# Top-64 attention with a three-step threshold search on one core: where GpSimd makes the second correction of a threshold

## The chip, the cores and the metric

The kernel runs on one core of a Trainium2 chip. A core has five engines that run side by side and meet only at semaphores: TensorE (PE in the profile) multiplies matrices, VectorE (DVE), ScalarE (ACT) and GpSimd (POOL) work on rows of on-chip memory, and SyncE (SP) issues transfers. Each engine runs its own instructions in the order in which the program hands them over. The metric is the time of one execution in microseconds (us), taken on the device; the times given are medians of several executions.

## What is computed

The reference takes x of 4 x 1024 x 256, applies half of a feed-forward layer, then attention, then half of the feed-forward layer again. Only the attention matters here. Cut to its core it reads:

```python
dots = jnp.einsum('bhid,bhjd->bhij', q, k) * QK_SCALE        # q and k normalised, 16 heads
dots = jnp.einsum('hg,bgij->bhij', W_pre_th, dots)           # heads mixed
dots = jnp.where(causal[None, None], mask_value, dots)       # 4 memory keys are always seen
vk = jax.lax.top_k(dots, TOPK)[0][..., -1:]                  # the 64th largest of a row
dots = jnp.where(dots < vk, mask_value, dots)
attn = jax.nn.softmax(dots, axis=-1)
attn = jnp.einsum('hg,bgij->bhij', W_post_th, attn)          # heads mixed again
out = jnp.einsum('bhij,bhjd->bhid', attn, v)
```

The hard part is `vk`: for each row of scores, its 64th largest value.

## The kernel before

Three stages run one after the other: a first stage (feed-forward and projections), the attention, and a last stage (feed-forward). The attention takes from about 905 us to about 3300 us of the profiled execution.

**Tiles and steps.** A tile is 8 queries of all 16 heads, so 128 rows, and as many columns as its last query can see: from 12 at the start of a sequence to 1028 at its end (`reach`, called n here). A sequence has 128 tiles, the four sequences have 512. A step k handles two tiles, an even and an odd one; there are 256 steps. Eight steps make a block of 128 queries, and eight blocks make a sequence. The widths grow from block to block and start again with the next sequence. Tiles with fewer than 76 columns need no search (`searched` is false for the first four steps of a sequence).

**The search.** ScalarE counts how many scores of a row lie above a guess: a pass of `Sign` over the tile with a running sum (line 1099, function `count(g, r)`, r from 0 to 3; each pass has a main instruction and a read of the sum). GpSimd turns the count into a better guess with two operations on 128 x 2 numbers: `move = cnt * factor` (line 1186), then, behind a semaphore on itself, `nt = move + base` (line 1187). This is `better(p, q)`, with q = 1, 2, 3 for the first, second and third correction. `better(p, q)` waits for both tiles' counts of round q-1, and ScalarE's counts of round q wait for its `nt`. After the fourth count (r = 3, written to `SG`) GpSimd works out how far off the count is and on which side (`off` and `sgn`, lines 1198 and 1200), and writes the scores with a sign and scaled to a tiny size into `W` (`signed(g)`, line 1209, the scaling pass, one per tile; this is the one wide pass of GpSimd in a step). VectorE puts the `SG` marks and `W` together (`sides(g)`, line 1354, one per tile, reading two arrays), takes the eight largest (`closest`, line 1361), and picks the right one (`picked`, lines 1369 and 1373). Then it cuts the exponentials at that threshold (`select`, line 1419).

**Which step works on which tiles.** The work is spread over steps by hand. In step k, ScalarE does in this order: the fourth counts of pair k-2, the copies `AT` of the mixed weights (line 1122) for the even tile of pair k-5, the second counts (r = 1) of pair k-1, the exponentials and copies of older pairs, the third counts (r = 2) of pair k-1, and the first counts (r = 0) of pair k. GpSimd does: third correction of pair k-2, first correction of pair k-1, the sides of pair k-2, two scaling passes of pair k-2, the second correction of pair k-1, then small work and two passes `kr` (line 1242), then the first guess of pair k (lines 1174 and 1180), which waits for VectorE's copies `D` of that pair (line 1340). VectorE does: `D` of pair k's even tile, `sides` of both tiles of pair k-2, `D` of the odd tile, `closest`, `picked`, and two `select`, with copies of new scores `Sn` (line 1329) in between. TensorE makes scores (lines 963 and 964), mixes heads (line 977), turns and mixes the weights (line 1004) and multiplies with the values (line 1032).

**What the scaling passes wait for.** `signed` of the even tile and of the odd tile wait for `sgn` and for the buffers `W` that `picked` has freed. `sides` of each tile waits for its own scaling pass through the semaphore `v`.

## Time and profile before

| | us |
|---|---|
| median of 3 executions | 3618.76 |
| lowest and highest of them | 3610.93 and 3638.0 |
| the profiled execution, its time | 3616.38 |
| the profiled execution, its span | 3614.0 |

The profile is of one execution. Its page gives for each engine the time in which it was busy, and groups of instructions with their count, busy time, mean duration and idle time just before them. The sum of the prediction is made against the 3616.38 us of the profiled execution; the median is 2.4 us (0.07%) above it. A row of the timeline begins with the start in us from the span's start and the duration in us; rows of one engine that follow each other with the same line are merged and counted (x2); where a pair is shown with x1 too, that answer was cut before the second began. Windows are given for three blocks of the third sequence, each of 8 steps from the start of the fourth counts of its first pair; a row has the window, its length, each engine's busy time with its count of instructions, and at the end the granted TensorE clock (1 is full), the share of DMA and its GB/s.

### The profile page before, as it was taken

What the parts mean: (1) busy time and instruction counts of PE and PEld (TensorE: products, weight loads), DVE (VectorE), ACT (ScalarE), POOL (GpSimd) and SP (SyncE); (2) the same over time, 40 slices, a digit from 0 to 9 for tenths busy, and PEclk for the clock granted to TensorE, in tenths of its full rate; (3) what the DMA queues carried; (4) which work ended last, traced back from release to release, by engine and by line L of the source; (5) the groups of instructions that cost most, each with busy time, mean ns of one, the idle gap of its engine ahead of it and who ended that gap; (6) DMA issues with size and microseconds to landing.
All of it is one profiled execution on the core that took longest, in us unless ns stands there. A gap on an engine that the chain in (4) does not pass through costs nothing. (4 is left out here: it accounts for less than half of the span.)

```text
span 3614.0 us, 73990 instructions
## 1 busy us (share of the span) xinstructions
PE 3186.2 (88%) x22950; PEld 2118.9 (59%) x22950; DVE 2795.0 (77%) x6342; ACT 2567.5 (71%) x5953; POOL 2380.7 (66%) x6267
## 2 busy tenths in 40 slices
PE   7999999997788898878999888889988899987898
PEld 4445454443556666755666665566676566666566
DVE  6677766667688999778999867899986888985354
ACT  3444544443688999778899967899986888896221
POOL 2666666655777767688776768776767876674232
PEclk9999999998699999989999998999998999999899
DMA  3223222224456665346666435566534566641110
GB/s 121 99 82 111 105 88 88 82 82 153 135 164 177 187 182 128 90 145 179 178 187 175 100 109 153 170 193 182 152 86 129 168 180 178 180 105 46 38 36 29
DMA packets 363391, 467.04 MB, mean 129 GB/s; under 512 B 29460, under 2 KB 295060, under 8 KB 362520
## 3 DMA queue, kind: packets, MB, share of 16 engines
q1 hardware_dynamic: 362904, 461.54, 43.5%
q8 instruction: 185, 3.03, 0.4%
q14 instruction: 302, 2.47, 0.3%
HBM read 227.09 MB, written 234.36 MB: 128 GB/s over the span
## 5 line engine op out<-in xcount | busy, mean ns | idle before, releaser
L1099 ACT ACTIVATE junk<-D,nt 128x76 int8<-128x76 f32 (+62 forms) x1440 | 1070.2, 747 | 98.4 <-POOL nt L1187 65.5
L1004 PE MATMUL banks<-kr,E 128*128 128x128 f32 (+1 forms) x4672 | 702.9, 299 | 111.1 <-ACT AT L1122 64.6
L1004 PEld LDWEIGHTS banks<-kr,E 128*128 128x128 f32 (+1 forms) x4672 | 602.2, 202 | 258.5 <-issue 154.2
L977 PE MATMUL banks<-Sg,kpre 128*128 128x109 f32 (+51 forms) x1568 | 603.6, 493 | 23.3 <-POOL maskb L1256 13.0
L1329 DVE COPY Sn<-banks 128x686 f32<-128x686 f32 (+11 forms) x440 | 375.9, 854 | 165.7 <-PE banks L964 130.2
L1354 DVE SCALAR_TENSOR_TENSOR W<-SG,sgn,W 128x76 f32<-128x76 int8 (+14 forms) x480 | 413.1, 900 | 104.1 <-POOL W L1209 103.5
L963 PE MATMUL banks<-kT,qT 64*128 64x343 f32 (+11 forms) x880 | 390.3, 525 | 103.6 <-DVE Sn L1329 97.5
L1122 ACT ACTIVATE AT<-banks 128x512 f32<-128x512 f32 (+3 forms) x768 | 344.8, 479 | 185.2 <-PE banks L1004 184.3
L585 DVE RECIPROCAL a_share<-a_share 128x512 f32<-128x512 f32 x128 | 419.9, 3324 | 70.3 <-POOL a_share L529 36.6
L1032 PE MATMUL banks<-AT,V 128*64 128x64 f32 x9216 | 392.8, 233 | 81.9 <-issue 71.5
L1032 PEld LDWEIGHTS banks<-AT,V 128*64 128x64 f32 x9216 | 323.1, 142 | 156.0 <-issue 138.1
L1419 DVE SCALAR_TENSOR_TENSOR E<-D,vk,E 128x12 f32<-128x12 f32 (+56 forms) x512 | 394.5, 779 | 3.1 <-ACT E L1109 1.5
L1099 ACT ACTIVATE SG<-D,nt 128x76 int8<-128x76 f32 (+14 forms) x480 | 357.0, 745 | 50.8 <-DVE hit L1369 48.4
L964 PE MATMUL banks<-kT,qT 64*128 64x343 f32 (+11 forms) x880 | 390.7, 526 | 0.0
L1209 POOL TENSOR_SCALAR W<-D,sgn 128x76 f32<-128x76 f32 (+14 forms) x480 | 376.2, 793 | 0.4
L1109 ACT ACTIVATE E<-D,least 128x12 f32<-128x12 f32 (+56 forms) x512 | 369.3, 721 | 9.6 <-POOL E L1236 6.5
L1340 DVE TENSOR_SCALAR_CACHE_REDUCE D<-banks 128x13 f32<-128x13 f32 (+62 forms) x504 | 339.4, 674 | 40.8 <-PE banks L981 40.3
L977 PEld LDWEIGHTS banks<-Sg,kpre 128*128 128x128 f32 x1568 | 267.0, 205 | 169.3 <-issue 116.2
L1186 POOL TENSOR_TENSOR move<-cnt,tab 128x2 f32<-128x2 f32 x720 | 224.0, 311 | 182.5 <-ACT junk L1099 177.8
L1361 DVE MAX8 m<-W 128x8 f32<-128x76 f32 (+14 forms) x480 | 326.7, 721 | 22.0 <-issue 19.5
L1099 ACT ACTIVATION_READ_ACCUMULATOR junk<-D,nt 128x1 f32 x1440 | 275.4, 191 | 0.0
L529 POOL TENSOR_SCALAR a_share<-a_share 128x512 f32<-128x512 f32 x128 | 190.3, 1487 | 122.0 <-ACT a_share L440 122.0
(195 smaller groups left out, 5710.8 us busy)
## 6 DMA issues: line engine op xcount, KB each, us to landing
score_scratch<-Sn SPq DMA_DIRECT2D x96, 343.0 KB, 3.4
q_scratch<-a_share SPq DMA_DIRECT2D x32, 512.0 KB, 2.7
v_scratch<-a_share SPq DMA_DIRECT2D x32, 512.0 KB, 3.6
k_scratch<-a_share SPq DMA_DIRECT2D x32, 512.0 KB, 2.7
gate_scratch<-a_share SPq DMA_DIRECT2D x32, 512.0 KB, 2.8
kT<-k_scratch SPq DMA_DIRECT2D x32, 512.0 KB, 4.8
gateT<-gate_scratch SPq DMA_DIRECT2D x32, 512.0 KB, 9.8
qT<-q_scratch SPq DMA_DIRECT2D x31, 512.0 KB, 6.4
```

The costliest lines, as they stand in the source:

```text
L585: nc.vector.reciprocal(ri[:, c % 2, :], rr[:, c % 2, :]).then_inc(s["inv"], 1)
L963: nc.tensor.matmul(ps[0][:, 0:c1 - c0], qT[0:DH, p, :], kT[0:DH, p, c0:c1], start=True, stop=True)
L964: nc.tensor.matmul(ps[1][:, 0:c1 - c0], qT[DH:P, p, :], kT[DH:P, p, c0:c1], start=True, stop=True).then_inc(s["s_ps"], 1)
L977: out = nc.tensor.matmul(bank[:, 0:c], kpre[:].rearrange("p h r -> p (h r)"), Sg[:, g % 3, c0:c1], start=True, stop=not diagonal)
L1004: out = nc.tensor.matmul(ps[5 + i % 2][0:rows, c % 4 * P:(c % 4 + 1) * P], E[:, g % 4, c * P:c * P + rows], kr[:, g % 4, :], start=True, s ...
L1032: out = nc.tensor.matmul(into, V[:, c, h * DH:(h + 1) * DH], rows, start=(c == 0), stop=(c == ib and (ib > 0 or hb % 2 == 0)))
L1099: nc.scalar.activation(out, D[:, e, 1:1 + n], ACT.Sign, bias=nt[:, r, e:e + 1], scale=-1.0, accum_out=cnt[:, r, e:e + 1]).then_inc(s[f"cnt ...
L1109: nc.scalar.activation(E[:, g % 4, 0:n], D[:, e, 1:1 + n], ACT.Exp, bias=least[:, e:e + 1], scale=-1.0).then_inc(s["exp"], 1)
L1209: ts(W[:, g % 2, 0:n], D[:, g % 8, 1:1 + n], sgn[:, g % 8:g % 8 + 1], -SMALL, ALU.mult, ALU.mult).then_inc(s["v"], 1)
L1329: nc.vector.tensor_copy(Sn[:, i % 2, :, 0:c1 - c0], banks[:, 0:2, 0:c1 - c0]).then_inc(s["s_sb"], 1)
L1354: nc.vector.scalar_tensor_tensor(out=W[:, h, 0:n], in0=SG[:, h, 0:n], scalar=sgn[:, e:e + 1], in1=W[:, h, 0:n], op0=ALU.is_equal, op1=ALU. ...
L1419: nc.vector.scalar_tensor_tensor(out=E[:, g % 4, 0:n], in0=D[:, g % 8, 1:1 + n], scalar=vk[:, g % 8:g % 8 + 1], in1=E[:, g % 4, 0:n], op0= ...
```

## The change

One call changes its place in GpSimd's step. The second correction of pair k-1 stood behind both scaling passes of pair k-2; now it stands between them.

```diff
                 if searched(k - 2):
                     signed(2 * (k - 2))
-                    signed(2 * (k - 2) + 1)
                 if searched(k - 1):
                     better(k - 1, 2)
+                if searched(k - 2):
+                    signed(2 * (k - 2) + 1)
                 if searched(k - 2):
                     distance(k - 2)
```

No instruction is added or removed, and no wait changes. What moves can be seen in GpSimd's order at two places of a sequence. The first is the step whose scaling passes are 188 and 196 columns wide (a difference, + is new):

```order
 L1192 TENSOR_TENSOR base<-nt,tab 128x2
 L1209 TENSOR_SCALAR W<-D,sgn 128x188
+L1186 TENSOR_TENSOR move<-cnt,tab 128x2
+L1187 TENSOR_TENSOR nt<-move,base 128x2
 L1209 TENSOR_SCALAR W<-D,sgn 128x196
-L1186 TENSOR_TENSOR move<-cnt,tab 128x2
-L1187 TENSOR_TENSOR nt<-move,base 128x2
 L1215 TENSOR_TENSOR pos<-off,sgn 128x2
 L1242 TENSOR_SCALAR kr<-kpost,rinv 128x128
```

The odd tile's scaling pass now stands behind two small operations, the first of which waits for ScalarE's second counts of the next pair. The same happens in every step with a search. At the step with passes of 492 and 500 columns, ScalarE's order, which is the same before and now, shows who waits for the moved `nt`: the two counts of 508 and 516 columns that follow the exponentials (`E`).

```order
L1099 ACTIVATE SG,cnt<-D,nt 128x492
L1099 ACTIVATE SG,cnt<-D,nt 128x500
L1122 ACTIVATE AT<-banks 128x64x8
L1099 ACTIVATE junk,cnt<-D,nt 128x508
L1099 ACTIVATE junk,cnt<-D,nt 128x516
L1109 ACTIVATE E<-D,least 128x476
L1122 ACTIVATE AT<-banks 128x64x8
L1109 ACTIVATE E<-D,least 128x484
L1099 ACTIVATE junk,cnt<-D,nt 128x508
L1099 ACTIVATE junk,cnt<-D,nt 128x516
```

The first pair of 508 and 516 is the second count (r = 1), which the moved correction reads; the last pair is the third count (r = 2), which waits for what it makes.

## Rows read from the trace of the kernel before

**Rows 1.** The page: busy us, share of the span and instructions of each engine
```profile
PE 3186.2 (88%) x22950; PEld 2118.9 (59%) x22950; DVE 2795.0 (77%) x6342; ACT 2567.5 (71%) x5953; POOL 2380.7 (66%) x6267
```
**Rows 2.** Waits of the whole span: us in total, times, longest us
```profile
ACT junk L1099 <- POOL nt L1187: 65.5, 98, 1.3
ACT AT L1122 <- PE banks L1004: 184.3, 149, 5.2
POOL move L1186 <- ACT junk L1099: 177.8, 287, 2.6
DVE W L1354 <- POOL W L1209: 103.5, 79, 2.5
```
**Rows 3.** Groups by line: busy us, mean ns | idle us before, releasers
```profile
L1187 POOL TENSOR_TENSOR nt<-move,base 128x2 f32<-128x2 f32 x720 | 227.6, 316 | 56.4
L1354 DVE SCALAR_TENSOR_TENSOR W<-SG,sgn,W 128x76 f32<-128x76 int8 (+14 forms) x480 | 413.1, 900 | 104.1 <-POOL W L1209 103.5
```
**Rows 4.** Windows, blocks 2, 4, 8: length, busy PE, PEld, DVE, ACT, POOL
```profile
2147.80:2202.10 54.30, 42.68 (x297) 30.77 (x294) 38.99 (x168) 41.05 (x161) 44.06 (x193) 0.78 0.49 142
2264.10:2334.40 70.30, 60.47 (x524) 41.95 (x522) 61.48 (x176) 60.44 (x161) 54.34 (x192) 0.95 0.60 174
2598.40:2686.10 87.70, 74.72 (x716) 58.25 (x715) 76.40 (x154) 85.79 (x154) 66.61 (x166) 0.92 0.41 98
```
**Rows 5.** GpSimd's and VectorE's waits in block 2 (2147.8 to 2202.1)
```profile
POOL move L1186 <- ACT junk L1099: 1.9, 1, 1.9
POOL nt L1174 <- DVE D L1340: 1.5, 3, 0.8
DVE W L1354 <- POOL W L1209: 4.7, 4, 2.0
```
**Rows 6.** VectorE's wait in block 8 (2598.4 to 2686.1)
```profile
DVE W L1354 <- POOL W L1209: 8.5, 6, 2.1
```
**Rows 7.** Timeline, a narrow step of block 2: GpSimd, then VectorE
```profile
2168.47 0.83 POOL L1209 TENSOR_SCALAR W<-D,sgn 128x188 f32<-128x188 f32 x2
2169.27 0.29 POOL L1186 TENSOR_TENSOR move<-cnt,tab 128x2 f32<-128x2 f32 x1
2169.85 0.19 POOL L1215 TENSOR_TENSOR pos<-off,sgn 128x2 f32<-128x2 f32 x1
2168.93 0.91 DVE L1354 SCALAR_TENSOR_TENSOR W<-SG,sgn,W 128x188 f32<-128x188 int8 x2 [1.18 <-POOL W L1209]
```
**Rows 8.** Timeline, a step of block 4: GpSimd, VectorE, ScalarE
```profile
2315.60 1.34 POOL L1209 TENSOR_SCALAR W<-D,sgn 128x492 f32<-128x492 f32 x2
2316.90 0.60 POOL L1186 TENSOR_TENSOR move<-cnt,tab 128x2 f32<-128x2 f32 x1
2317.58 0.57 POOL L1187 TENSOR_TENSOR nt<-move,base 128x2 f32<-128x2 f32 x1
2316.31 1.14 DVE L1354 SCALAR_TENSOR_TENSOR W<-SG,sgn,W 128x492 f32<-128x492 int8 x1 [1.66 <-POOL W L1209]
2316.31 1.79 DVE L1354 SCALAR_TENSOR_TENSOR W<-SG,sgn,W 128x492 f32<-128x492 int8 x2 [1.66 <-POOL W L1209]
2315.86 0.19 ACT L1099 ACTIVATION_READ_ACCUMULATOR junk<-D,nt 128x1 f32 x1
2318.19 0.72 ACT L1099 ACTIVATE junk<-D,nt 128x508 int8<-128x508 f32 x1 [0.49 <-POOL nt L1187]
```
**Rows 9.** Timeline, the last step of block 4: GpSimd, then VectorE
```profile
2323.78 1.36 POOL L1209 TENSOR_SCALAR W<-D,sgn 128x508 f32<-128x508 f32 x2
2327.72 0.19 POOL L1186 TENSOR_TENSOR move<-cnt,tab 128x2 f32<-128x2 f32 x1 [2.58 <-ACT junk L1099]
2329.55 1.41 DVE L1354 SCALAR_TENSOR_TENSOR W<-SG,sgn,W 128x508 f32<-128x508 int8 x2
```
**Rows 10.** Timeline, a wide step of block 8: GpSimd, VectorE, ScalarE
```profile
2651.19 2.14 POOL L1209 TENSOR_SCALAR W<-D,sgn 128x972 f32<-128x972 f32 x2
2652.30 3.19 DVE L1354 SCALAR_TENSOR_TENSOR W<-SG,sgn,W 128x972 f32<-128x972 int8 x2 [2.08 <-POOL W L1209]
2653.18 0.18 ACT L1099 ACTIVATION_READ_ACCUMULATOR junk<-D,nt 128x1 f32 x1
2656.77 0.19 POOL L1174 TENSOR_TENSOR nt<-D,tab 128x2 f32<-128x2 f32 x1 [0.22 <-DVE D L1340]
2658.41 1.11 ACT L1099 ACTIVATE junk<-D,nt 128x1004 int8<-128x1004 f32 x1
```

## The prediction

> **What bounds the kernel now.** The page first: TensorE is busy for 88% of the span, VectorE 77%, ScalarE 71%, GpSimd 66% [rows 1]. These are means over three stages. The change touches the attention alone, so I read that next, block by block, in the view of windows [rows 4]. Block 2 of a sequence (narrow tiles) takes 54.3 us for 8 steps: GpSimd is the busiest with 44.06 us, and the view of waits gives it only 1.9 + 1.5 us of waiting [rows 5]; the other 7 us are the gaps of its semaphores on itself. So GpSimd's own string of small operations sets the pace there. Block 4 takes 70.3 us, with TensorE, VectorE and ScalarE all at 60 to 61 us and GpSimd at 54: no engine is full, the pace comes from how they wait for each other. Block 8 takes 87.7 us with ScalarE at 85.79: there ScalarE is the bound. The view of waits over the span then says what is to be had and what is at stake [rows 2]: ScalarE waits 65.5 us in 98 places for a corrected threshold `nt`, which can be any of the three corrections, and VectorE waits 103.5 us in 79 places for a scaling pass.
>
> **What one step does, worked out at three widths.** The timeline of a step in block 4 shows the mechanism [rows 8]. The two scaling passes take 1.34 us, .67 each. VectorE's `sides` of the even tile is issued at 2316.31, just behind the even pass (2316.27), but takes 1.14 us and ends at 2317.45; a pair of `sides` of about that width with no GpSimd pass beside it takes 1.41 us, so .7 each [rows 9]. It stood still until the odd scaling pass ended at 2316.94. The small operations suffer the same way from the other side: `move` should take .19 us as in [rows 9] and takes .60, until 2317.50, .05 us behind the end of `sides`; `nt` takes .57. So a GpSimd operation and a `sides` exclude each other, whole instruction by whole instruction, and who comes first goes first. The Trainium skill says the same in "SBUF — State Buffer", section "SBUF: two separate sides": the port pair that both share is an exclusive lock held for the whole instruction; this trace agrees. That page also has a blocked GpSimd operation go on about 115 ns behind VectorE's end, where the row above shows 50; by its figure each of the handovers below would cost .07 us more, two in a step where VectorE waits.
>
> In the new order the same step goes: even pass to 2316.27; the second counts of the next pair were read at 2315.86 + .19 = 2316.05, so `move` waits for nothing and ends at about 2316.46; `sides` even takes the freed turn and ends at about 2316.46 + .51 = 2316.97 (.51 is what it took from 2316.94 to 2317.45); `nt` slips in behind it, about 2317.03 instead of 2317.58 + .57 = 2318.15; the odd pass ends at about 2317.72; `sides` odd at about 2318.28 instead of 2316.31 + 1.79 = 2318.10. So three things move: ScalarE's third count, which waited .49 us, waits no more; GpSimd is through its three operations and two passes about .4 us sooner; and VectorE is through `sides` .2 us later, now idle in the middle.
>
> At the narrow width [rows 7] the same walk gives: even pass to 2168.89, `move` to 2169.08, `sides` even about .27 to 2169.35, `nt` to 2169.40, odd pass .41 to 2169.81, so `pos` at about 2169.8 against 2169.85. The gain of GpSimd is .05 us, or .15 if `sides` is quicker than I scale it; I take .1.
>
> At the wide width [rows 10] the second counts are read only at 2653.18 + .18 = 2653.36, while the even pass ended at 2652.26. Now the moved wait holds the odd pass behind it: `move` and `nt` take to about 2653.85, the odd pass (1.07) to 2654.92, `sides` odd to about 2656.0 against 2652.30 + 3.19 = 2655.49, so .5 us later. What is late next is `D` of the odd tile and then GpSimd's first guess, at 2656.77 now. Its count starts on ScalarE at 2658.41, 1.4 us behind the guess's end at 2656.96, so .5 us of delay fits under the counts that ScalarE has to do anyway.
>
> **The sum.** Four terms, for the four sequences.
> 1. Narrow steps, about 10 in a sequence where GpSimd sets the pace, 40 in all, .1 us each: -4 us. The row of `nt` bounds it: its mean is 316 ns [rows 3] against the .19 us of an undisturbed small operation [rows 9], over 720 of them .126 x 720 = 91 us, of which a third, the second corrections, 30 us, and as much for `move`: 60 us if all blocking went and all of it lay on the path. The other end is 0: in 3 steps of block 2 GpSimd waits for `D` behind all this [rows 5], which comes no sooner.
> 2. ScalarE's waits for `nt`, 65.5 us at most [rows 2]. Nothing keeps them on the path: in block 4 ScalarE has 10 us of idle time in 70, and the next thing that it waits for is TensorE's work for `AT`, 184.3 us in all; what it gains at the third count it gives back there unless TensorE is fed sooner. Ends 0 and -65.5. I take a tenth, -6 us, since the blocks with the longest of these waits are those in which GpSimd, VectorE or TensorE sets the pace.
> 3. VectorE's later end of `sides`, where it was waiting for them: 79 places [rows 2], .2 us in the middle and .5 in wide ones, so 79 x .5 = +40 us at the most. In block 8 there are 6 in this sequence [rows 6], 24 in four, covered by ScalarE as worked out above; in block 2 there are 4 [rows 5], 16 in four, where GpSimd sets the pace. The other 39 at .3 make 12 us, and I take half of it, +6 us, since VectorE's next wait is often for TensorE.
> 4. Where VectorE comes late to `sides`, nothing is lost: GpSimd is through before. The last step of a block is the sharpest case [rows 9]: `move` waited 2.58 us for the counts, until 2327.72, and the odd pass, which ended at 2325.14, will now end at about 2327.72 + .19 + .28 + .69 = 2328.9. VectorE starts that pair of `sides` at 2329.55. The cover is .7 us; without it up to 3 us a block, 32 blocks, 96 us. I take 0.
>
> Together -4 - 6 + 6 = -4 us, so 3616.4 - 4 = 3612 us, 0.2% under the median of 3618.8. A measurement of this kernel can tell about 1% (36 us) from no change.
>
> **The rivals.**
> A. ScalarE's waits for `nt` are on the path after all, and most of them come back. For it: 98 waits, in the blocks in which all engines have gaps; ScalarE would run ahead and feed the next counts sooner. Against it: TensorE and VectorE are as busy as ScalarE in block 4 [rows 4]. All of it gives 3616 - 65.5 = 3551, half of it 3583. Chance .2, of which .13 beyond 1%.
> B. Slower. The moved wait holds the odd scaling pass, VectorE stands at `sides` odd with its `D`, `closest` and `select` queued behind, and TensorE and ScalarE wait for those. Price: 79 x .5 = 40 us, 3656. It decides as soon as each waiting step costs over .46 us (36 / 79) with no cover, or as the cover of .7 us in the last step of a block [rows 9] is used up. For it: GpSimd waits 177.8 us for counts at `move`, 287 times, so they are often not there when it asks, though these are all three corrections. Against it: the wide steps, where it costs .5, have 1.4 us of slack. Chance .17, of which .11 beyond 1%.
> C. The change does nothing because the counts arrive no sooner than the end of the odd pass. In block 8 the second counts come 1.1 us behind the even pass, the length of the odd one, and ScalarE does not wait for `nt`: there it is so. In the narrow and middle steps it is not [rows 8]. 3616 to 3619, chance .08.
>
> **How the numbers follow.** The forecast of small terms that nearly cancel has .55. Its own range is 3598 to 3630: term 2 at twice its value and term 1 at three times on one side, term 3 at its full 12 us and a few more on the other. The range for 8 in 10 reaches into A and B: 3586 to 3646. It leaves out about .11 of A and .07 of B. Faster by over 1% (under 3583): A's .13. Slower by over 1% (over 3655): B's .11. Within 1%: the rest, .76.
>
> **What would show it.** ScalarE's wait for `nt` of line 1187 falls from 65.5 us to under 20, and its wait for TensorE at `AT` rises from 184 by a good part of that: term 2. The mean of `sides` falls from 900 ns to about 750, since it no longer stands still inside the odd pass, and VectorE's wait for a scaling pass rises from 103.5 us to 150 or more, now with waits before odd tiles too: term 3. The mean of `nt` falls below 316 ns. GpSimd's wait for counts at `move` rises from 177.8 us. Block 2 gets shorter by about 1 us, block 8 keeps its 87.7 us within half a us. It is wrong if block 4 changes by more than 1.5 us, if block 8 gets longer, or if the last step of a block shows VectorE waiting at `sides` odd.

## The result, and the profile after

The change costs 0.6%. The median after is 3642.56 us (four executions, 3640.32 to 3644.83) against 3619.22 us before (four, 3610.93 to 3638.0); the ratio is 1.0057 with a 95% interval of 1.0033 to 1.0082, so 12 to 30 us. It lies inside the range of the prediction and within its band of 1%, but on the other side of zero: 4 us of gain were forecast, 23 us of loss came. The profiled execution took 3641.57 us with a span of 3639.3 (before 3616.38 and 3614.0).

The page of the kernel after, busy time of each engine (as [rows 1]), and from its groups by line (busy us, mean ns | idle us before, releasers; from line 1285 on, every line number is one higher than before) those that answer to [rows 3] and three more:

```profile
PE 3193.4 (88%) x22950; PEld 2120.6 (58%) x22950; DVE 2760.9 (76%) x6342; ACT 2572.7 (71%) x5953; POOL 2413.3 (66%) x6267
...
L1187 POOL TENSOR_TENSOR nt<-move,base 128x2 f32<-128x2 f32 x720 | 176.7, 245 | 56.3
L1355 DVE SCALAR_TENSOR_TENSOR W<-SG,sgn,W 128x76 f32<-128x76 int8 (+14 forms) x480 | 391.4, 834 | 200.7 <-POOL W L1209 200.1
L1242 POOL TENSOR_SCALAR kr<-kpost,rinv 128x128 f32<-128x128 f32 x512 | 311.7, 609 | 29.6 <-DVE rinv L1427 29.5
L1099 ACT ACTIVATE junk<-D,nt 128x76 int8<-128x76 f32 (+62 forms) x1440 | 1070.5, 746 | 117.2 <-POOL nt L1174 94.8 <-POOL nt L1187 18.8
L1099 ACT ACTIVATE SG<-D,nt 128x76 int8<-128x76 f32 (+14 forms) x480 | 356.9, 744 | 73.9 <-DVE hit L1370 72.8
```

The corrections got quicker (`nt` 316 to 245 ns) and so did `sides` (900 to 834 ns), but VectorE's idle time in front of `sides` went from 104.1 to 200.7 us. Busy and idle together, `sides` took 413.1 + 104.1 = 517 us of VectorE before and 592 us now: 75 us more, of which 23 reached the end. The row of `kr` is one that the prediction had left out: this pass, which stands behind the odd scaling pass, had 215.5 us and a mean of 422 ns before. Of the 206 waits before `sides`, 79 stand before the even tile, as many as before, and 127 before the odd tile, where there was none.

The waits of the whole span after (us, times, longest), as [rows 2]:

```profile
ACT AT L1122 <- PE banks L1004: 159.1, 143, 3.8
POOL move L1186 <- ACT junk L1099: 172.4, 288, 3.3
DVE W L1355 <- POOL W L1209: 200.1, 206, 2.3
ACT junk L1099 <- POOL nt L1174: 94.8, 144, 14.8
ACT junk L1099 <- POOL nt L1187: 18.8, 35, 1.0
ACT SG L1099 <- DVE hit L1370: 72.8, 113, 2.0
```

and three of the kernel before that the prediction did not use:

```profile
ACT junk L1099 <- POOL nt L1174: 29.6, 45, 14.2
ACT SG L1099 <- DVE hit L1369: 48.4, 80, 1.7
POOL nt L1174 <- DVE D L1340: 129.5, 99, 4.8
```

ScalarE's wait for a correction (`nt` of line 1187) fell from 65.5 to 18.8 us, as meant. But its wait for the first guess (`nt` of line 1174) rose from 29.6 to 94.8, and its wait for VectorE's `hit` from 48.4 to 72.8. So ScalarE starts its third counts sooner and then stands still at the first counts. VectorE's wait for a scaling pass rose to 200.1 us, in 206 places where there were 79.

Blocks 2, 4 and 8 of the third sequence after (length, busy PE, PEld, DVE, ACT, POOL; as [rows 4]):

```profile
2169.20:2223.70 54.50, 42.83 (x297) 30.64 (x296) 38.34 (x169) 41.14 (x161) 45.61 (x192) 0.81 0.50 141
2285.50:2355.90 70.40, 60.31 (x524) 41.86 (x522) 60.48 (x177) 60.64 (x162) 55.89 (x192) 0.95 0.59 174
2619.80:2709.90 90.10, 73.55 (x714) 57.02 (x712) 72.84 (x157) 86.43 (x152) 68.61 (x166) 0.92 0.39 95
```

Block 2 is .2 us longer, block 4 .1, block 8 2.4. GpSimd is busy 1.5 us more in each of the first two.

Three steps tell how. The step of block 4 with passes of 492 and 500 columns after, which answers to [rows 8] (start us, duration us, engine, line; in brackets the idle time before and what ended it):

```profile
2338.09 0.68 POOL L1209 TENSOR_SCALAR W<-D,sgn 128x492 f32<-128x492 f32 x1
2338.74 0.20 POOL L1186 TENSOR_TENSOR move<-cnt,tab 128x2 f32<-128x2 f32 x1
2338.81 0.73 DVE L1355 SCALAR_TENSOR_TENSOR W<-SG,sgn,W 128x492 f32<-128x492 int8 x1 [1.25 <-POOL W L1209]
2339.01 0.58 POOL L1187 TENSOR_TENSOR nt<-move,base 128x2 f32<-128x2 f32 x1
2339.58 0.68 POOL L1209 TENSOR_SCALAR W<-D,sgn 128x500 f32<-128x500 f32 x1
2340.22 0.19 POOL L1215 TENSOR_TENSOR pos<-off,sgn 128x2 f32<-128x2 f32 x1
2340.29 0.74 DVE L1355 SCALAR_TENSOR_TENSOR W<-SG,sgn,W 128x500 f32<-128x500 int8 x1 [0.75 <-POOL W L1209]
2340.39 0.87 POOL L1242 TENSOR_SCALAR kr<-kpost,rinv 128x128 f32<-128x128 f32 x1
```

Counted from the start of the even pass, `sides` of the odd tile ends at 2340.29 + .74 - 2338.09 = 2.94 us; before, at 2316.31 + 1.79 - 2315.60 = 2.50. That is .44 us later where the prediction had .2. Behind it GpSimd's `kr` pass now overlaps `sides` odd and takes .87 us.

The narrow step of block 2 with passes of 188 and 196 columns after, as [rows 7]:

```profile
2190.48 0.43 POOL L1209 TENSOR_SCALAR W<-D,sgn 128x188 f32<-128x188 f32 x1
2191.79 0.19 POOL L1215 TENSOR_TENSOR pos<-off,sgn 128x2 f32<-128x2 f32 x1
2191.86 0.42 DVE L1355 SCALAR_TENSOR_TENSOR W<-SG,sgn,W 128x196 f32<-128x196 int8 x1 [0.50 <-POOL W L1209]
2191.96 0.56 POOL L1242 TENSOR_SCALAR kr<-kpost,rinv 128x128 f32<-128x128 f32 x1
```

`pos` stands 2191.79 - 2190.48 = 1.31 us behind the start of the even pass, before it was 1.38: the .07 us that term 1 counted on are there, and `kr` takes them and more (.56 us, before .36). `sides` odd ends 1.80 us behind that start against 1.37, so .43 us late, much as in block 4.

The wide step with passes of 972 and 980 columns after, as [rows 10]; `SG` is the end of its fourth counts:

```profile
2671.35 1.05 POOL L1187 TENSOR_TENSOR nt<-move,base 128x2 f32<-128x2 f32 x1
2672.07 0.19 ACT L1099 ACTIVATION_READ_ACCUMULATOR SG<-D,nt 128x1 f32 x1
2674.12 1.08 POOL L1209 TENSOR_SCALAR W<-D,sgn 128x972 f32<-128x972 f32 x1
2675.51 1.01 POOL L1186 TENSOR_TENSOR move<-cnt,tab 128x2 f32<-128x2 f32 x1 [0.31 <-ACT junk L1099]
2677.89 1.24 DVE L1355 SCALAR_TENSOR_TENSOR W<-SG,sgn,W 128x980 f32<-128x980 int8 x1 [1.43 <-POOL W L1209]
2677.99 1.38 POOL L1242 TENSOR_SCALAR kr<-kpost,rinv 128x128 f32<-128x128 f32 x1
2680.40 0.19 POOL L1174 TENSOR_TENSOR nt<-D,tab 128x2 f32<-128x2 f32 x1 [0.52 <-DVE D L1341]
2680.63 1.13 ACT L1099 ACTIVATE junk<-D,nt 128x1004 int8<-128x1004 f32 x1
```

`sides` odd ends 5.01 us behind the start of the even pass, before 4.30. The first guess ends at 2680.59 and its count begins at 2680.63: of the 1.45 us that lay between them before [rows 10], .04 are left. Two rows of the kernel before, the end of the same fourth counts and the third count of this step, tell where they went:

```profile
2650.01 0.18 ACT L1099 ACTIVATION_READ_ACCUMULATOR SG<-D,nt 128x1 f32 x1
2656.20 1.10 ACT L1099 ACTIVATE junk<-D,nt 128x988 int8<-128x988 f32 x1
```

Behind the end of the fourth counts ScalarE's first counts begin at 8.22 us before (2658.41 - 2650.19) and 8.37 after (2680.63 - 2672.26), nearly the same. But the even pass begins at 1.00 before and 1.86 after, and the guess ends at 6.77 and 8.33. So GpSimd is .86 us late already when the step's passes begin, and .70 more are added in the step. The .86 come from the step before: VectorE's two `select`, which read two arrays as `sides` does, now fall later, and the second (2671.14 to 2672.34) blocks GpSimd's first correction (`nt`, 1.05 us above; .19 us before, at 2649.04).

**The mean over the steps.** Worked out from all records of the two traces, over the 222 steps whose neighbours have searches too, in us behind the end of a pair's fourth counts, which is the start of a step's work:

| | before | after |
|---|---|---|
| even scaling pass ends | 2.12 | 2.19 |
| second correction ends | 3.98 | 3.07 |
| odd scaling pass ends | 2.89 | 3.80 |
| `sides` odd ends | 4.68 | 5.05 |
| first guess ends | 5.97 | 6.16 |
| `hit` ends | 7.78 | 8.04 |
| third counts begin | 4.65 | 4.31 |
| first counts begin | 6.23 | 6.22 |
| the next step's fourth counts begin | 7.98 | 8.08 |

The third counts begin .34 us sooner, the first counts do not, since their guess is .19 us later; and the next step is .10 us later. Times 222 that is 22 us, about the whole loss.

**By block.** From one pair's fourth counts to the next, summed over the four sequences, the profiled execution after is longer than the one before by these us (22.9 together):

| block | 1 | 2 | 3 | 4 | 5 | 6 | 7 | 8 |
|---|---|---|---|---|---|---|---|---|
| after less before | 1.2 | .1 | 8.4 | 2.2 | .5 | -3.8 | 6.1 | 8.1 |

So blocks 3, 7 and 8 make the loss, and block 6 gains.

### The profile page after: what moved, and what is told of

Its sections match the earlier page's. It is cut to its first block and busy times, and to the rows that moved or that the text cites. A ratio compares the mean times of both kernels' runs of the same rounds, so it can differ in the third digit from the quotient of the medians.

```text
span 3639.3 us, 73990 instructions
## 1 busy us (share of the span) xinstructions
PE 3193.4 (88%) x22950; PEld 2120.6 (58%) x22950; DVE 2760.9 (76%) x6342; ACT 2572.7 (71%) x5953; POOL 2413.3 (66%) x6267
## 5 line engine op out<-in xcount | busy, mean ns | idle before, releaser
L1099 ACT ACTIVATE junk<-D,nt 128x76 int8<-128x76 f32 (+62 forms) x1440 | 1070.5, 746 | 117.2 <-POOL nt L1174 94.8
L1355 DVE SCALAR_TENSOR_TENSOR W<-SG,sgn,W 128x76 f32<-128x76 int8 (+14 forms) x480 | 391.4, 834 | 200.7 <-POOL W L1209 200.1
L1122 ACT ACTIVATE AT<-banks 128x512 f32<-128x512 f32 (+3 forms) x768 | 344.0, 477 | 160.1 <-PE banks L1004 159.1
L1099 ACT ACTIVATE SG<-D,nt 128x76 int8<-128x76 f32 (+14 forms) x480 | 356.9, 744 | 73.9 <-DVE hit L1370 72.8
L1032 PEld LDWEIGHTS banks<-AT,V 128*64 128x64 f32 x9216 | 322.6, 142 | 147.9 <-issue 128.6
L1242 POOL TENSOR_SCALAR kr<-kpost,rinv 128x128 f32<-128x128 f32 x512 | 311.7, 609 | 29.6 <-DVE rinv L1427 29.5
L1186 POOL TENSOR_TENSOR move<-cnt,tab 128x2 f32<-128x2 f32 x720 | 206.8, 287 | 178.1 <-ACT junk L1099 172.4
```

Source lines behind the costliest of these rows:

```text
L1032: out = nc.tensor.matmul(into, V[:, c, h * DH:(h + 1) * DH], rows, start=(c == 0), stop=(c == ib and (ib > 0 or hb % 2 == 0)))
L1099: nc.scalar.activation(out, D[:, e, 1:1 + n], ACT.Sign, bias=nt[:, r, e:e + 1], scale=-1.0, accum_out=cnt[:, r, e:e + 1]).then_inc(s[f"cnt ...
L1355: nc.vector.scalar_tensor_tensor(out=W[:, h, 0:n], in0=SG[:, h, 0:n], scalar=sgn[:, e:e + 1], in1=W[:, h, 0:n], op0=ALU.is_equal, op1=ALU. ...
```

## Experiments

Three theories stood at the start (their letters have nothing to do with those of the rivals above). **V**: VectorE comes late through `sides` odd, and what is queued behind it (`D`, `closest`, `hit`) holds ScalarE. **G**: GpSimd's `kr` pass, now blocked by `sides` odd, makes the first guess late, and that alone costs. **C**: the passes are held by the moved wait for the second counts. The ratios below are against the kernel before on the same chip, with 95% intervals. A step below is counted as in the table of means, from the end of a pair's fourth counts.

### The wait alone, and each half of the blocks

The kernel before, with nothing but the wait of the moved correction between the two passes:

```diff
                     signed(2 * (k - 2))
+                    if searched(k - 1):
+                        pool.wait_ge(s["cnt1"], 2 * FP[k - 1] + 2)
                     signed(2 * (k - 2) + 1)
```

> The kernel before, with one wait more: between the two scaling passes GpSimd waits for the second counts of the next pair, and the correction stays behind both passes. Theory C: this holds the odd pass as the change does, so most of the 23 us appear, 3630 to 3645, above all in blocks 7 and 8, where the counts come 0.3 to 1 us behind the even pass. Theories V and G in their form that the loss comes from the handovers between sides, the correction and kr: in blocks 1 to 5 the counts are there already, nothing changes; in blocks 7 and 8 sides even gets its turn in the wait, so some of it appears; 3618 to 3628.

3622.86 us, 0.9999 [0.9984, 1.0015]. Its waits:

```profile
DVE W L1356 <- POOL W L1209: 147.9, 131, 2.5
...
POOL W L1209 <- ACT junk L1099: 92.9, 105, 3.9
```

GpSimd stands 92.9 us at the odd pass, and nothing comes of it: the steps in which the pass is held by the counts are not those that cost. C falls as the cause of the whole. It also shows that 44 us more of waiting at `sides` (147.9 against 103.5) can be free, with a `sides` odd that ends .07 us later in the mean step.

The new order in blocks 7 and 8 alone, and, with `< 48` in place of `>= 48`, in blocks 1 to 6 alone:

```diff
+                between = (k - 2) % 64 >= 48
                 if searched(k - 2):
                     signed(2 * (k - 2))
+                    if not between:
+                        signed(2 * (k - 2) + 1)
                 if searched(k - 1):
                     better(k - 1, 2)
-                if searched(k - 2):
+                if searched(k - 2) and between:
                     signed(2 * (k - 2) + 1)
```

> The new order in blocks 7 and 8 of each sequence alone, the old one in blocks 1 to 6. Summed over steps of the two profiles the change costs 6 us in block 7 and 6.5 in block 8, plus about 4 in the steps at the turn of a sequence. If the cost of a block is its own: 3628 to 3636. If it is made elsewhere and only shows there: under 3624.

> The new order in blocks 1 to 6 alone, the old one in blocks 7 and 8. By the two profiles blocks 1 to 6 cost 1 + 0 + 8 + 2 + 1 - 4 = 8 us together: 3622 to 3630. Theory C says that nothing is lost where counts are there in time, so about 3619.

Blocks 7 and 8: 3631.78 us, 1.0034 [1.0018, 1.005]. Blocks 1 to 6: 3626.67 us, 1.0019 [1.0003, 1.0035]. The two losses of some 12 and 7 us add up to 19, near the 23 of the whole. The loss is not one of a single place. That the widest quarter of the steps has the larger part is likely, and the table by block says so, but the two intervals overlap.

### The repairs that V and G ask for

V says that `D` of the odd tile should not stand behind `sides` odd. So the new order with VectorE's `D` between its two `sides`:

```diff
                     sides(2 * (k - 2))
-                    sides(2 * (k - 2) + 1)
                 if k < S:
...
+                if searched(k - 2):
+                    sides(2 * (k - 2) + 1)
```

> The new order, and on VectorE the copy D of the odd tile of pair k ahead of sides of the odd tile of pair k-2, instead of behind it. Theory V (VectorE's path): the change costs its 23 us because sides odd now starts only when the late odd scaling pass is through, and D, the first guess and ScalarE's first count stand behind it; then D first fills VectorE's hole of 0.5 to 1.4 us, ScalarE's wait for the first guess (94.8 us) falls below 40 and the time comes back to 3615 to 3625. Theory G (GpSimd's path: the even kr pass stands still inside sides odd, 797 ns instead of 440, and the first guess stands behind it): kr still collides with sides odd, so at most a third comes back, 3635 to 3643. Theory C (the odd pass is held for the second counts): nothing comes back in the wide blocks.

3637.05 us, 1.0052 [1.0033, 1.0071]: 2 us better than the change by the ratios, 5 by the medians, which is not to be told from nothing. VectorE's wait for the passes fell to 117.5 us, and another took its place, for TensorE's sums (`flag`), 7 us in the kernel after:

```profile
DVE W L1355 <- POOL W L1209: 117.5, 116, 2.5
...
DVE flag L1337 <- PE banks L991: 94.3, 120, 3.7
```

This is a miss for V as it stood: it asked for 3615 to 3625 us and for ScalarE's wait for the first guess below 40 us, and that wait is 101.4 us. The trace shows why the test is weak. `sides` odd now ends later still (5.9 us into the step), the even `kr` pass is blocked by it as before (a mean of 569 ns, 797 after the change, 440 before), and GpSimd comes to the guess .69 us behind the end of `D` (.15 after the change). The run traded one hold-up for another.

The same edit on the old order is the control.

> The control to D first: the old order on GpSimd, and D of the odd tile between the two sides on VectorE. With the new order this took 5 us off. Here VectorE has no hole between its sides. Theory V: D and the first guess come 0.7 us sooner but sides odd, closest and picked later, 3615 to 3625. If D first costs by itself, because VectorE stands waiting for TensorE (95 us of waiting before flag in the run with the new order, 7 without), 3625 to 3635, and then it gave back more than 5 us in that run.

3640.97 us, 1.0072 [1.0054, 1.009]. So the repair costs 28 us by itself, above the range for it too, yet does not worsen the new order. V can live with that (the edit takes in one place what it gives back in another), but neither run speaks for V.

The `D` of the odd tile ahead of both `sides`, old order:

```diff
-                if searched(k - 2):
-                    sides(2 * (k - 2))
-                    sides(2 * (k - 2) + 1)
                 if k < S:
...
+                if searched(k - 2):
+                    sides(2 * (k - 2))
+                    sides(2 * (k - 2) + 1)
```

> The old order on GpSimd, and on VectorE D of the odd tile ahead of both sides. D reads the matmul's banks, not the shared port, so it can run beside the two scaling passes, in the time in which sides even stands still. If VectorE's standing still in sides even (1007 ns against 793 of sides odd, 51 us over 240 steps) is worth something, this is faster than both kernels, 3590 to 3615; if TensorE does not have the odd tile ready by then, VectorE waits for it with both sides behind, and it is slower, 3625 to 3650.

3747.16 us, 1.0358 [1.0332, 1.0384]. `flag` waits 342.2 us for TensorE; the wait for the passes is down to 12.1 us. It is far above both ranges named for it. Both places of the odd `D` ahead of the old one are worse.

G says that the guess must come ahead of `kr`. The new order with the first guess moved up:

```diff
-                if 0 <= k - 4 < S:
-                    spread(2 * (k - 4))
                 if searched(k - 1):
                     based(k - 1, 2)
-                if 0 <= k - 4 < S:
-                    spread(2 * (k - 4) + 1)
                 if searched(k):
...
+                if 0 <= k - 4 < S:
+                    spread(2 * (k - 4))
+                if 0 <= k - 4 < S:
+                    spread(2 * (k - 4) + 1)
```

> The new order, and on GpSimd the first guess of the next pair (lines 1174 and 1180) ahead of both kr passes instead of behind them. Theory G: the even kr pass, 797 ns instead of 440 because it stands still inside sides odd, holds the first guess and so ScalarE's first count (wait 94.8 us); with the guess in front of it the loss goes, 3619 to 3627. Theory V (sides odd itself is late, and D behind it): the guess has to wait for D anyway, kr is now held behind that wait, and the time stays at 3640 or gets worse, with TensorE waiting for kr.

3675.15 us, 1.0153 [1.0129, 1.0176], about 1% worse than the change. The guess has nothing before it and still ends 6.21 us into the step (6.16 after the change), because it waits for `D`:

```profile
POOL nt L1174 <- DVE D L1341: 298.0, 233, 17.5
```

So G falls: `kr` is stretched by half, but the guess was waiting for VectorE anyway. The trace of the kernel after says the same without the edit: there the guess begins .15 us behind the end of `D` in the mean (.25 before), and within .1 us of it in 163 of 232 steps (129 before). The control, the same edit on the old order:

> The control for the run before: the old order with the first guess ahead of both kr passes. Theory G: there kr hardly stood still (440 and 403 ns), so moving the guess changes little, 3612 to 3622. Theory V: the same. If this order costs by itself, for kr then waits behind D and TensorE behind kr, this run shows the cost and it has to be taken off the run before.

3628.24 us, 1.0033 [1.0015, 1.0051]; there the guess does come sooner (5.83 against 5.97), and the edit costs 11 us all the same, above the 3612 to 3622 us expected; that the late `kr` is the reason is not shown.

Both repairs on the new order:

> The new order with both repairs: D odd ahead of sides odd on VectorE, and the first guess ahead of kr on GpSimd. D first alone gave back 5 of 23 us (3637). If the first guess is what the loss runs through, by D and by kr together, both repairs give back more than their sum, 3612 to 3622. If the loss runs through sides odd itself to closest, picked and select, nothing more comes back than by D first, 3635 to 3645.

3642.95 us, 1.0067 [1.004, 1.0093]: as the change alone. ScalarE's wait for the first guess fell to 38.3 us, near the 29.6 of the old order, its wait for `hit` stayed at 73.7, and the time did not come back. By what was expected that speaks for a loss through `closest`, `picked` and `hit`, and not through the guess; but each repair costs time of its own in the old order (28 and 11 us), so the run doesn't decide it. It was run on another chip than the first repair, so it doesn't tell their shares.

### VectorE late, with GpSimd's order as it was

The cleanest test of V leaves GpSimd's order alone and puts a dead operation between VectorE's two `sides`, a `MAX8` over 384 columns whose result is overwritten:

```diff
                     sides(2 * (k - 2))
+                    nc.vector.max(m8[:, 2 * (k - 1) % 8, :], kpost[:].rearrange("p h r -> p (h r)").unsqueeze(1).broadcast_to([P, 3, H * R8]))
                     sides(2 * (k - 2) + 1)
```

> The old order; between the two sides of a step VectorE does one more operation of 384 columns that nothing reads (about 0.45 us by the row of MAX8, 0.72 us at 550 columns). It does not touch the port that GpSimd shares. So VectorE is through its pair of sides later by about what the change makes it (0.37 us in the mean of a step), and GpSimd's order is as before. Theory V (the cost of the change is only that VectorE ends its pair of sides later): 3636 to 3650. If the cost is made on GpSimd's side (kr, late scaling pass), then VectorE's gaps of over 1 us a step take this up: 3619 to 3626.

3655.16 us, 1.0115 [1.0098, 1.0132], so 42 us. Its groups and waits:

```profile
L1471 DVE MAX8 m<-kpost 128x8 f32<-128x384 f32 x240 | 132.0, 550 | 0.0
L1242 POOL TENSOR_SCALAR kr<-kpost,rinv 128x128 f32<-128x128 f32 x512 | 289.8, 567 | 32.2 <-DVE rinv L1426 31.6
...
ACT SG L1099 <- DVE hit L1369: 69.9, 115, 2.0
ACT junk L1099 <- POOL nt L1174: 69.7, 147, 14.9
```

The old order shows every sign of the change as soon as VectorE is late: `kr` 567 ns, ScalarE waiting for the first guess in 147 places (144 after the change) and for `hit` in 115 (113). In the mean of the steps the second correction even ends sooner than before (3.78), but `sides` odd ends at 5.16, the guess at 6.24, `hit` at 8.10, the next step begins at 8.14. So the stretched `kr` is a consequence of a late `sides` odd; that a late VectorE costs time is shown here, with `kr`'s part in it. That the inserted operation does not itself block GpSimd is in the traces: `MAX8` reads one operand, and in the kernel before GpSimd's `move` takes .19 us while one runs (2319.78). The Trainium skill, "SBUF — State Buffer", section "SBUF: two separate sides", has a VectorE operation take the shared port when it has two inputs in SBUF or runs in a two-port mode. The trace agrees: `sides` has two and excludes GpSimd (`move` .60 us in [rows 8]), `MAX8` has one and does not (.19).

The same with 128 columns, to see whether the price is proportional:

```diff
                     sides(2 * (k - 2))
+                    nc.vector.max(m8[:, 2 * (k - 1) % 8, :], kpost[:].rearrange("p h r -> p (h r)"))
                     sides(2 * (k - 2) + 1)
```

> The delay of VectorE between its two sides once more, with 128 columns in place of 384, so about 0.2 us in place of 0.45. Theory V with no slack at all: in proportion, 3630 to 3638. If the pair of sides has some slack in most steps, the small delay costs much less than in proportion, 3613 to 3624.

3629.48 us, 1.0019 [1.0007, 1.0031], so 7 us, for 283 ns of `MAX8` and a `sides` odd that ends .23 us later. With .48 us later and 42 us above, the first quarter of a us is nearly free and the next costs. A straight line between the two gives for the change's .37 us a loss of 7 + (.37 - .23) / (.48 - .23) x 35 = 27 us; 23 were measured. That is an estimate over two points, and its fit is in part luck, for by block the two kinds of delay do not cost the same (us over four sequences, as in the table by block):

| block | 1 | 2 | 3 | 4 | 5 | 6 | 7 | 8 |
|---|---|---|---|---|---|---|---|---|
| `MAX8` of 384 columns | 1.1 | 3.8 | 3.1 | 1.8 | 12.2 | 10.4 | 4.3 | 1.6 |
| the change | 1.2 | .1 | 8.4 | 2.2 | .5 | -3.8 | 6.1 | 8.1 |

In part this is how late `sides` odd is: in blocks 5 and 6 it ends .64 and .54 us later by the `MAX8`, .18 and .05 by the change. But in block 3 the two are about equally late (.33 and .38) and the change costs nearly three times as much, and in block 8 (.85 and 1.21) five times as much. So a late `sides` odd is a cause; that it is the only one is not shown. These are single profiled executions; with the new order in blocks 7 and 8 alone, blocks 1 to 6 differ by up to 1.5 us each from the kernel before, which gives a measure of the scatter.

### What the split costs, and what the early correction is worth

In the old order, the operation `pos`, which stands behind the passes with a wait of GpSimd on itself, put between them; the correction stays behind both:

```diff
                     signed(2 * (k - 2))
+                    distance(k - 2)
+                    pool.wait_ge(s["pos"], FP[k - 2] + 1)
                     signed(2 * (k - 2) + 1)
...
-                if searched(k - 2):
-                    distance(k - 2)
```

> The old order of the corrections, but the small operation pos (line 1215), which GpSimd did behind them anyway, stands between the two scaling passes, with a wait for its end, so that VectorE's sides even gets its turn there. The pair of passes is split as in the change; the correction does not come early and no count is waited for. Theory of the split: sides odd ends about 0.3 us later as in the change, and the time goes up by as much as by the change or more, since ScalarE gets nothing for it: 3638 to 3655. If the early correction itself does harm (ScalarE ahead of the others), this run stays at 3619 to 3626.

3644.28 us, 1.0082 [1.0066, 1.0099], so 31 us without any early correction. VectorE stands at the passes in 232 places, and ScalarE's wait for the correction grows too:

```profile
DVE W L1354 <- POOL W L1209: 193.1, 232, 2.5
...
ACT junk L1099 <- POOL nt L1187: 111.2, 124, 1.6
```

Here `sides` odd ends only .18 us later (4.86), but the correction .31 us later (4.29). The next test takes that apart: the correction later and the passes not. In the old order GpSimd's `base` for the second correction (line 1192) goes from ahead of the passes to behind them:

```diff
-                if searched(k - 1):
-                    based(k - 1, 1)
                 if searched(k - 2):
                     signed(2 * (k - 2))
...
                 if searched(k - 1):
+                    based(k - 1, 1)
                     better(k - 1, 2)
```

> The old order, but the small operation base1 (line 1192, 0.2 us), which stood ahead of both scaling passes, stands behind them, ahead of the second correction that needs it. Both passes and VectorE's pair of sides come 0.18 us sooner, the correction by nothing, GpSimd's work is the same. Theory V says that the time follows the end of the pair of sides in both directions: by the run with VectorE's delay (42 us for 0.45 us) up to 16 us less, so 3598 to 3613, with ScalarE's waits for hit and for the first guess lower. If the end of sides has slack on this side, so that only a delay counts: 3613 to 3620.

I had meant it to bring the passes forward. It did not: they end .02 us sooner, because most of the .19 us of `base` lay in the gap behind `sgn`, for which the pass waits (`sgn` ends at 2168.34, the pass begins at 2168.47 in the narrow step of the kernel before). Behind the passes it is blocked by `sides`, and the correction ends .36 us later (4.34). 3640.31 us, 1.0054 [1.0036, 1.0072]:

```profile
L1192 POOL TENSOR_TENSOR base<-nt,tab 128x2 f32<-128x2 f32 x480 | 164.6, 343 | 0.3
```

So a correction that comes .36 us later costs 17 to 20 us (with it the first guess comes .10 us later, so the price is not of the correction alone). What one that comes .91 us sooner brings, as in the change, no run measures: the estimate above would leave 4 us for it, and that is within its error.

The correction ahead of both passes, which needs no split:

```diff
-                if searched(k - 2):
-                    signed(2 * (k - 2))
                 if searched(k - 1):
                     better(k - 1, 2)
                 if searched(k - 2):
+                    signed(2 * (k - 2))
                     signed(2 * (k - 2) + 1)
```

> The second correction ahead of both scaling passes. The two passes are neighbours again, so sides even stands still inside the odd pass as in the kernel before, and nothing of the pair of sides is split; but both passes come later by the correction (0.47 us) and, in blocks 7 and 8, by the wait for the counts. Theory of the handovers (the loss is the split of the pair: three turns one after the other where there were two): no third turn here, so less lost than by the change in blocks 1 to 6, and a total of 3622 to 3635. Theory C: both passes held, worse than the change, over 3650.

3751.08 us, 1.0379 [1.0352, 1.0406], far above the 3622 to 3635 us that the theory of the handovers gave; it lies where C had put it (over 3650). The wait for the counts now holds both passes, and the even one ends 3.47 us into the step in place of 2.12:

```profile
POOL move L1186 <- ACT junk L1099: 313.7, 373, 2.6
...
ACT junk L1099 <- POOL nt L1174: 203.6, 196, 13.7
DVE W L1354 <- POOL W L1209: 250.1, 185, 4.1
```

### One instruction in place of two with a wait between

Perhaps the new place would pay with a correction that needs no semaphore between `move` and `nt`. It was written as one operation for each tile, with the factor and the base as pointers, in both orders:

```diff
-                chain(tt(move[:, q - 1, e], cnt[:, q - 1, e], tab[:, G1 + q - 1, t], ALU.mult))
-                tt(nt[:, q, e], move[:, q - 1, e], base[:, q - 1, e], ALU.add).then_inc(s[f"nt{q}"], 1)
+                for i in range(2):
+                    c, d = e.start + i, t.start + i
+                    last = ts(nt[:, q, c:c + 1], cnt[:, q - 1, c:c + 1], tab[:, G1 + q - 1, d:d + 1],
+                              base[:, q - 1, c:c + 1], ALU.mult, ALU.add)
+                last.then_inc(s[f"nt{q}"], 1)
```

> The old order; each correction is made by one operation for each of the two tiles (count times factor plus base, 128 x 1) instead of move and then nt on both tiles behind a semaphore on itself. GpSimd loses three waits on itself in a step, and the third count's threshold comes sooner with the pair of passes unsplit. The run with base1 behind the passes made that threshold 0.36 us later and cost 20 us. If the time follows the threshold in this direction too, 3590 to 3610; if only the end of VectorE's pair of sides counts, 3610 to 3622.

> The same with the new order. Two short operations back to back leave VectorE no gap in which sides even gets its turn ahead of nt, if the second is already waiting when the first ends; then the odd pass is held by only 0.3 us and one handover less. By theory V the change's cost of 23 us falls to 5 to 15 us against the run with the old order and the same operations. If VectorE still gets its turn between them, the cost stays at 20 us or more against that run.

Old order 3691.96 us, 1.0206 [1.0174, 1.0238]; new order 3722.55, 1.0285 [1.0257, 1.0314]. The two are 31 us apart, so the new place costs no less with this correction than with the old one, though no semaphore stands between its two operations: VectorE gets its turn all the same. And the form is dear, where a gain or no change had been expected. In the old order:

```profile
L1188 POOL TENSOR_SCALAR nt<-cnt,tab,base 128x1 f32<-128x1 f32 x1440 | 735.7, 520 | 133.4 <-ACT junk L1099 128.2 <-DVE hit L1372 1.0
```

1440 x 520 ns = 736 us stand where `move` and `nt` had 224 + 228 us and 56 us of gaps between them. No kernel that was run is clearly faster than the old order.

## Why the prediction was wrong

The step that failed is term 3 of the sum, VectorE's later end of `sides`: it was put at +6 us, with the wide steps of block 8 at nothing because ScalarE was to cover them. The runs showed 127 new waits before `sides` odd, 75 us more of VectorE's time at `sides`, and a loss of 23 us, of which blocks 7 and 8 have 14 by the profiles. Terms 1 and 2, together -10 us, did not come through to the end either. That the time stayed within 1% is no credit to the sum.

**What bounds the kernel** was read rightly, and so was the first part of the mechanism: a scaling pass and a `sides` exclude each other, `sides` even takes the freed turn, the correction slips in behind it, and VectorE is through later. Rival B had the mechanism of the loss, VectorE standing at `sides` odd with `D`, `closest` and `select` queued behind. It got .17 and a price of 40 us; 23 us are 60% of that.

**Term 3 failed in its price, its count and its cover.** The time of one was too small: .2 us in the middle was .44, .5 in the wide step was .7, and the narrow step, where I had none, lost .43. The prediction timed `sides` odd behind the odd pass with .56 us, from a `sides` that had been issued and was standing blocked (.51 us of it behind the block's end). But VectorE waits for the odd pass through a semaphore, is idle, and only then issues: .03 us for the semaphore and .74 for the whole operation, 2341.03 - 2340.26 = .77 us. This .21, and .05 that had come together up to the end of the odd pass, make the .26 between the .18 of the walk and the .44. The number of places was too small: 79 was the count of waits in the old order, where the odd pass comes straight behind the even one and never lets VectorE wait a second time. The new order adds 127 before the odd tile, 206 in all. The cover in the wide steps is answered under term 2. The last factor, that half is given back, was not too kind: of 75 us more on VectorE 23 reached the end. In the wide step the end of the odd pass, 3.74 us behind the start of the even one, came out as walked (3.73), but by luck: the counts were there .87 us sooner than in [rows 10], since GpSimd was late itself, and `sides` even, which had begun in the wait, then blocked `move` for most of its 1.01 us.

**Term 4 was right in its sharpest case and too broad.** In the last step of block 4 (as [rows 9]):

```profile
2349.18 0.20 POOL L1186 TENSOR_TENSOR move<-cnt,tab 128x2 f32<-128x2 f32 x1 [0.95 <-ACT junk L1099]
2349.63 0.70 POOL L1209 TENSOR_SCALAR W<-D,sgn 128x516 f32<-128x516 f32 x1
2351.00 1.54 DVE L1355 SCALAR_TENSOR_TENSOR W<-SG,sgn,W 128x508 f32<-128x508 int8 x2
```

The odd pass ends at 2350.33 and VectorE comes at 2351.00: the .7 us of cover are there. But the odd pass ends .91 us later in the mean step, and each VectorE that used to come within these .91 us without waiting now waits. "Nothing is lost" held at the end of this block and not in the steps before it.

**Term 2 was right in its event and wrong in what follows.** The wait fell below 20 us, to 18.8. I let ScalarE give the gain back at `AT`, for TensorE; that wait fell too, from 184.3 to 159.1. It gave it back one pass further on, at the first counts, for the guess, which hangs on `D` and so on `sides` odd. In blocks 4 to 6 ScalarE had waited at the third count in 44 of 96 steps and now does in none, so it comes to the first counts sooner than the guess. [Rows 10] had 1.45 us of slack at the first counts in a wide step, and I took it as cover for .5 us of delay. There ScalarE had not waited for the third count; the slack went on GpSimd's side. The walk ended with the step. It counted the .5 us added in it (.70 measured) and not the .86 us by which GpSimd came late into it, held by a later `select`. The two make 1.56 us, more than the slack.

**Term 1** was .07 us a step as computed, and was spent in the next instruction. GpSimd's `kr` pass stands right behind the three small operations. In the old order `sides` odd had ended by then (`kr` .36 us); now it has just been issued, and `kr` takes .56 us in the narrow step, .87 in block 4 and 1.38 in the wide one. The delayed `MAX8` kernel shows this without the change. I had walked the step to `pos` and stopped there. The bound of the term was misread too. It gave the second corrections a third of the blocking, 30 us at `nt`; but they had most of it (a mean of 488 ns, against 263 and 197 for the first and third), and `nt` fell by 51 us and `move` by 17. `kr` rose by 96.

**Of the signs**, the wait for `nt`, the mean of `nt` (245 ns), the wait of VectorE above 150 us and block 4 within 1.5 us came as told. The mean of `sides` came to 834 ns and not 750, the wait at `move` fell a little (177.8 to 172.4) where it was to rise, block 2 got .2 us longer in place of 1 us shorter, and block 8 grew by 2.4 us: that was named as a sign of error, and it was one.

**What stays open.** How the 23 us divide. The split alone costs 31 us in one form, with a correction .31 us later; a correction .36 us later costs 17 to 20; a VectorE .48 us later costs 42. These don't add up in a straight line, and no run has the split's effect on VectorE with the correction at its old time. Whether the lateness of VectorE reaches ScalarE by the guess or by `hit` is open: both waits rose, and the repairs took each of them back by itself (the guess to 38.3 us with both repairs, `hit` to 48.1 with `D` first) without the time coming back. Why the change costs more in blocks 3 and 8 than a `MAX8` that makes VectorE about as late is open, and so is what the early correction brings.

## What to carry to other kernels

Where two engines exclude each other on a port, two long operations back to back hide a handover: the consumer of the first is issued while it is blocked and its successor finds its data ready. A small operation put between them lets the consumer in between, with a semaphore behind it or without, so the consumer starts from idle twice, and everything behind the second is late. Count the waits of the new order by walking a step past its last moved instruction into the next one on each engine; a count of waits, and a slack, read from the old order do not bound those of the new one (79 waits became 206, 1.45 us of slack became .04). A step that ends late also begins late the next time: ask which long operation of the late engine now falls on a short one of the other.

## What the hardware showed that I had not expected

- `sides` of 492 columns takes .73 us from its own issue, and .51 us measured from the end of the operation that blocked it: .2 us of it lie under the block. At 972 columns it is 1.23 us.
- A small GpSimd operation that `sides` blocks ends .05 us behind it: `nt` at 2339.59, `sides` at 2339.54, and a median of .05 us over 332 such cases in the trace before. The `kr` pass, some .36 us by itself, ends .23 us behind (2341.26 against 2341.03; a median of .24 over 207 cases in the trace after). The Trainium skill, in the section named above, gives about 115 ns from VectorE's end to the end of the block, for a transfer that GpSimd issues; the small operation here was through in less than half of that.
- GpSimd's operation with two pointer operands on 128 x 1 numbers has a median of 336 ns and a mean of 520 over the span with the old order, against .19 us for an undisturbed operation of two tensors on 128 x 2.
